# Building two adjacency matrices: 32 source blocks of 100 columns in place of 40 of 80, laps of 8 groups in place of 12

## The chip, the cores and the metric

The kernel runs on one core of one Trainium2 chip. The metric is device time in microseconds (us) of one execution. In this text PE is TensorE (PEld its weight loads), DVE is VectorE, ACT is ScalarE, POOL is GpSimd and SP is SyncE. A trailing q (DVEq, PEldq, SPq) means the instruction queue of the engine: register, branch, semaphore and DMA-issuing instructions, which are not counted as busy.

## The reference

A graph of 3125 nodes with 128 features and 103125 edges (sorted by destination) goes through four layers, each followed by an add and a layer norm: a weighted graph convolution, a graph attention layer with four heads, a dense attention over edges, and two mean aggregations with a hidden layer between. Cut to what matters here:

```
def _L0_gnn_ref(x, edge_row, edge_col, edge_val, weight, b):
    xw = x @ weight
    msgs = edge_val[:, None] * xw[edge_col]
    out = jax.ops.segment_sum(msgs, edge_row, num_segments=N_NODES)
    return jax.nn.relu(out + b)
...
x = _layernorm(x + _L0_gnn_ref(x, src, dst, edge_weight, ...))
x = _layernorm(x + _L1_gnn_ref(x, edge_index, ...))
x = _layernorm(x + _L2_gnn_ref(x, ..., edge_index))
x = _layernorm(x + _L3_gnn_ref(x, edge_index, ...))
```

All four layers sum over the edges of each destination. The kernel turns the edge list once into two dense matrices of 3200 x 3200 f32 in DRAM, row = destination and column = source: the number of edges, and the sum of their weights. Every layer then works from these.

## The kernel before, in words

`edge_tables` (L107) reads the edge list, and for every *group* of WD = 3 destination rows fetches 128 consecutive edges from the group's first edge on, one edge to a partition. Its loop over BATCHES (L331 to L338) unpacks them into the bf16 table `near`: for each group a field "key" (destination in the group times HI plus source block, 0 to KEYS-1), a field "low" (column in the block, 0 to SL-1), and the edge's weight split into PARTS = 3 bf16 numbers.

`build_matrices` (L420) makes the matrices. A row of 3200 columns is cut into HI = 40 source blocks of SL = 80, so a group of three rows has KEYS = 120 keys. The matrix product over the 128 edges of (one-hot of the key) and (one-hot of low, and the same times each part of the weight) gives a group's three rows as 120 partitions of 80 columns, for counts and weights at once. LW = 12 groups make a lap, and there are LAPS = 88 laps, run as a hardware loop of 44 with two laps in its body (`each_lap`, L445). Each lap goes through five engines:

- VectorE (`onehots`, L474): waits until the buffers of two laps ago are used, compares a grid with "low" for all 12 groups (L484, 960 elements), compares a grid with the key (L486, 1440 elements), waits for the first of the two, and multiplies by the three parts (L490, three times 960).
- TensorE (`products`, L517): per group three multiplications with the same stationary key one-hots of 128 columns (120 and 8 of zeros): moving 160 columns (low and first part), 80 and 80. The last of the lap's 36 is held back and issued after `beyond`.
- Between a lap's work and the next, VectorE's queue and TensorE's queue run `beyond` (L454): load two entries of the table `before_row` (L452), compare them and branch (L457). Only where a group has more than 128 edges is more work done; in this data the branch is never taken.
- ScalarE (`copy_out`, L556): copies the lap from PSUM into one of two staging buffers (L558), once the stores from that buffer have landed.
- SyncE (`store`, L565): two DMAs per lap (L568), counts and weights, each from 120 partitions with 12 runs of 80 f32 (320 bytes).

PSUM, the one-hot buffers and the staging buffers are all double. The order between the engines is set by the semaphores `used`, `lows`, `made`, `copied` and `stored`; nothing else runs in this stage. The 32 rows that the laps don't cover are zeroed by a separate DMA. The next stage (`aggregate`, L667) starts when the last store has landed.

Of the kernel before, what the change touches and what calls it, by code (L numbers as in the profile page):

```python
# [14 lines left out]
BF16 = mybir.dt.bfloat16  # L15
I32 = mybir.dt.int32
I16 = mybir.dt.int16
# [4 lines left out]
P = 128  # L22
# [23 lines left out]
WD = 3  # L46
HI = 40
SL = NP // HI
KEYS = WD * HI
LW = 12  # L50
LAPS = NP // (WD * LW)
ROWS = LAPS * LW * WD
# [54 lines left out]
def edge_tables(nc, k):  # L107

    with ExitStack() as ctx:
# [61 lines left out]
        N_PADS = 4  # L171
        N_CONSTS = 17
        BT = WT // BATCHES
# [35 lines left out]
        def _(pool):  # L209
# [10 lines left out]
            pool.memset(wrap[:, :], 0.0).then_inc(consts, 1)  # L220
            pool.memset(k.KEY[:, :, :, KEYS:P, :], 0.0).then_inc(consts, 1)
            pool.memset(k.zeros[:, :], 0.0).then_inc(consts, 1)
            pool.wait_ge(consts, 9)
            pool.affine_select(out=k.ident[:, :], in_=k.ident[:, :], compare_op=ALU.not_equal, fill=1.0,
# [8 lines left out]
            pool.iota(edge_i[:, :], pattern=[[P, ECOL]], base=0, channel_multiplier=1).then_inc(consts, 1)  # L233
            pool.iota(k.low_grid[:], pattern=[[1, SL], [0, 2]], base=0, channel_multiplier=0).then_inc(consts, 1)
            pool.iota(k.key_grid[:], pattern=[[1, KEYS], [0, 2]], base=0, channel_multiplier=0).then_inc(consts, 1)
            pool.wait_ge(rows_ready, 1)
# [11 lines left out]
            pool.iota(k.iota_low[:, :], pattern=[[1, SL]], base=0, channel_multiplier=0)  # L248
            pool.iota(k.iota_key[:, :], pattern=[[1, P]], base=0, channel_multiplier=0)
            pool.memset(nought[:, :], 0.0).then_inc(noughts, 1)  # L250

        @block.vector
        def _(dve):
# [166 lines left out]
def build_matrices(nc, k):  # L420


    with ExitStack() as ctx:
# [8 lines left out]
        more_key = sb("bm_more_key", [P, P], BF16)  # L432
# [3 lines left out]
        used, lows, made, copied, more_step, more_made, more_used = map(  # L436
            sem, ("bm_used", "bm_lows", "bm_made", "bm_copied", "bm_more_step", "bm_more_made", "bm_more_used"))
        stored = [sem(f"bm_stored{s}") for s in range(2)]
# [34 lines left out]
        def _(dve):  # L473
            dve.sem_inc(more_used, 1)  # L474

            def onehots(lap, u, two):
                wide_low, wide_key = [P, LW // 2, SL, 2], [P, LW // 2, KEYS, 2]

                def spread(f, wide):
                    return (k.near[:, f, bass.ds(lap * LW, LW)].rearrange("p (a b) -> p a b", b=2).unsqueeze(2)  # L480
                            .to_broadcast(wide))

                dve.wait_ge(used, lap + 1)
                dve.tensor_tensor(OH[:, u, :, 0], k.low_grid[:].unsqueeze(1).to_broadcast(wide_low),  # L484
                                  spread(1, wide_low), ALU.is_equal).then_inc(lows, 1)
                dve.tensor_tensor(k.KEY[:, u, :, 0:KEYS], k.key_grid[:].unsqueeze(1).to_broadcast(wide_key),  # L486
                                  spread(0, wide_key), ALU.is_equal)
                dve.wait_ge(lows, lap + 1)
                for v in range(PARTS):
                    last = dve.tensor_tensor(OH[:, u, :, 1 + v], OH[:, u, :, 0], spread(2 + v, wide_low), ALU.mult)  # L490
                last.then_inc(made, 1)

                def more(at, w, c, b, i):
# [3 lines left out]
                    dve.tensor_scalar(more_key[:], k.iota_key[:], k.key_base[:, bass.ds(w, 1)],  # L497
                                      k.col_key[:, bass.ds(c, 1)], ALU.add, ALU.is_equal).then_inc(more_step, 1)
# [13 lines left out]
        @block.tensor  # L512
        def _(pe):
            pe.sem_inc(used, RING)
            pe.sem_inc(copied, 2)

            def products(lap, u, two):  # L517
                def place(i, v):
                    b, c = divmod(i, PER_BANK)
                    return ps[:, 4 * u + b, c * WIDE + SL * (v > 0):(c + 1) * WIDE]  # L520

                def body(i, planes):
                    a, b = divmod(i, 2)
                    for v in planes:
                        moving = OH[:, u, a, 0:2, :, b] if v == 0 else OH[:, u, a, 1 + v, :, b]
                        last = pe.matmul(place(i, v), k.KEY[:, u, a, :, b], moving, start=i % PER_BANK == 0 and v == 0,  # L526
                                         stop=True, skip_group_check=True)
                    return last

                pe.wait_ge(copied, lap + 1)  # L530
                pe.wait_ge(made, lap + 1)
                for i in range(LW - 1):
                    body(i, range(PARTS))
                body(LW - 1, range(PARTS - 1))

                def more(at, w, c, b, i):
                    pe.wait_ge(more_made, at + 1)
                    for v in range(PARTS):
                        out = ps[:, bass.ds(b + 4 * u, 1), bass.ds(i * WIDE + SL * (v > 0), WIDE - SL * (v > 0))]
                        out = out.rearrange("p b c -> p (b c)")  # L540
                        last = pe.matmul(out, more_key[:], more_oh[:, 0:2] if v == 0 else more_oh[:, 1 + v],
                                         start=False, stop=True, skip_group_check=True)
# [1345 lines left out]
def program(nc, ins, out):  # L1888
# [15 lines left out]
    with ExitStack() as ctx:  # L1904
# [6 lines left out]
        with ExitStack() as edges:  # L1911
# [14 lines left out]
            k.iota_low = esb("iota_low", [P, SL], I16)  # L1926
            k.iota_key = esb("iota_key", [P, P], I16)
            k.low_grid = esb("low_grid", [P, SL, 2], I16)
            k.key_grid = esb("key_grid", [P, KEYS, 2], I16)
            k.KEY = esb("key_onehots", [P, RING, LW // 2, P, 2], BF16)  # L1930
            edge_tables(nc, k)
# [52 lines left out]
```

## Time and profile before

| | us |
|---|---|
| median of 3 runs (2443.68 to 2446.11) | 2445.59 |
| the profiled execution, its own time | 2446.72 |
| its span, first to last instruction | 2445.0 |
| TensorE busy | 1906.3 (78%) |
| VectorE busy | 1752.6 (72%) |
| ScalarE busy | 1135.5 (46%) |
| GpSimd busy | 137.2 (6%) |

The span is what the rows divide up; 1.7 us of the execution's own time lie outside it. The mean granted clock of TensorE is 0.894 of its full speed. The busy shares are averages over many stages; the build of the matrices is the stretch between about 80 and 478 us.

### The profile page before, as it was taken

What the parts mean: (1) busy time and instruction counts of PE and PEld (TensorE: products, weight loads), DVE (VectorE), ACT (ScalarE), POOL (GpSimd) and SP (SyncE); (2) the same over time, 40 slices, a digit from 0 to 9 for tenths busy, and PEclk for the clock granted to TensorE, in tenths of its full rate; (3) what the DMA queues carried; (4) which work ended last, traced back from release to release, by engine and by line L of the source; (5) the groups of instructions that cost most, each with busy time, mean ns of one, the idle gap of its engine ahead of it and who ended that gap; (6) DMA issues with size and microseconds to landing.
All of it is one profiled execution on the core that took longest, in us unless ns stands there. A gap on an engine that the chain in (4) does not pass through costs nothing. (4 is left out here: it accounts for less than half of the span.)

```text
span 2445.0 us, 44627 instructions
## 1 busy us (share of the span) xinstructions
PE 1906.3 (78%) x16121; PEld 1450.0 (59%) x16122; DVE 1752.6 (72%) x1874; ACT 1135.5 (46%) x1959; POOL 137.2 (6%) x225
## 2 busy tenths in 40 slices
PE   3456666499478888888888898873899999598794
PEld 2455555355357666666666776662688887354452
DVE  4777777400349999999999999846788876572374
ACT  1244444200156777667777776642666665101001
POOL 4000000000000000000000000000000000010120
PEclk7787777799789999999999999996899999699897
DMA  3599999997013333212333311220433330492492
GB/s 103 108 210 210 210 210 210 228 355 258 6 54 110 110 110 109 76 47 97 109 109 109 109 67 50 78 62 18 172 134 107 134 108 3 179 413 115 201 420 77
DMA packets 336138, 341.99 MB, mean 140 GB/s; under 512 B 267785, under 2 KB 318369, under 8 KB 319825
## 3 DMA queue, kind: packets, MB, share of 16 engines
q1 hardware_dynamic: 333712, 338.62, 43.0%
q0 software_dynamic: 720, 1.77, 0.3%
q10 hardware_dynamic: 1648, 0.83, 0.1%
q8 instruction: 37, 0.61, 0.1%
q14 instruction: 21, 0.16, 0.0%
HBM read 214.18 MB, written 127.01 MB: 140 GB/s over the span
## 5 line engine op out<-in xcount | busy, mean ns | idle before, releaser
L1201 ACT ACTIVATE exponentials<-gr_ps,att_cols 128x256 f32<-128x256 f32 (+1 forms) x1300 | 495.8, 490 | 203.0 <-PE gr_ps L1091 201.0
L1091 PE MATMUL gr_ps<-ident,gr_r 128*128 128x128 f32 x2500 | 381.4, 292 | 66.6 <-DVE gr_r L1309 64.4
L1122 PE MATMUL gr_ps<-exponentials,heads 128*33 128x128 f32 x5000 | 364.8, 277 | 15.3 <-DVE exponentials L1316 15.3
L1091 PEld LDWEIGHTS gr_ps<-ident,gr_r 128*128 128x128 f32 x2500 | 282.9, 146 | 150.7 <-issue 128.7
L1316 DVE SCALAR_TENSOR_TENSOR exponentials<-exponentials,gr_count_t 128x3072 f32<-128x3072 f32 (+1 forms) x104 | 349.6, 3361 | 22.4 <-ACT exponentials L1201 18.3
L526 PE MATMUL bm_ps<-bm_oh,key_onehots 128*128 128x80 bf16 (+1 forms) x3168 | 237.2, 243 | 163.9 <-issue 140.4
L1282 DVE CUSTOM_DVE_ANT_0 gr_unread<-gr_src_rows,gr_closed 128x3125 bf16<-128x3125 f32 (+1 forms) x100 | 344.6, 3446 | 15.1 <-ACT gr_closed L1194 14.5
L526 PEld LDWEIGHTS bm_ps<-bm_oh,key_onehots 128*128 128x128 bf16 x3168 | 210.6, 115 | 190.7 <-issue 178.9
L1122 PEld LDWEIGHTS gr_ps<-exponentials,heads 128*33 128x33 f32 x5000 | 255.0, 111 | 83.1 <-issue 56.8
L558 ACT ACTIVATE bm_stage<-bm_ps 120x1920 f32<-120x1920 f32 x88 | 155.8, 1771 | 249.4 <-DMA adjacency<-bm_stage 225.7
L790 PE MATMUL sage_ps<-sage_counts,sage_parts 128*128 128x400 bf16 x1200 | 207.7, 337 | 13.6 <-DVE sage_counts L824 13.6
L1309 DVE TENSOR_SCALAR gr_r<-gr_src_rows,gr_lift_u,gr_floor_u 128x3125 f32<-128x3125 f32 (+1 forms) x100 | 186.7, 1908 | 14.0 <-PE gr_ps L1091 8.4
L790 PEld LDWEIGHTS sage_ps<-sage_counts,sage_parts 128*128 128x128 bf16 x1200 | 118.7, 99 | 103.2 <-DVE sage_counts L824 15.1
L1542 PE MATMUL ar_ps<-KT,ar_left 128*128 128x400 f32 x400 | 147.1, 512 | 13.7 <-DVE ar_low_u L1633 12.1
L490 DVE TENSOR_TENSOR bm_oh<-bm_oh,near 128x960 bf16<-128x960 bf16 x264 | 157.5, 652 | 0.0
L1561 PEld LDWEIGHTS ar_ps<-ar_pt,X 128*128 128x128 f32 x1250 | 147.1, 194 | 11.5 <-ACT ar_pt L1605 4.5
L1561 PE MATMUL ar_ps<-ar_pt,X 128*128 128x128 f32 x1250 | 149.4, 277 | 0.0
L695 PE MATMUL agg_gcn_ps<-agg_gcn_ring,agg_gcn_left 128*128 128x400 f32 x400 | 136.0, 504 | 4.6 <-DMA agg_gcn_ring<-adjacency 4.6
L484 DVE TENSOR_TENSOR bm_oh<-low_grid,near 128x960 bf16<-128x960 int16 x88 | 58.0, 659 | 101.9 <-PE bm_ps L526 93.1
L824 DVE CAST sage_counts<-sage_ring 128x3200 bf16<-128x3200 f32 x50 | 93.7, 1874 | 46.4 <-POOL sage_ring L780 46.4
L1605 ACT ACTIVATE ar_pt<-ar_ps 128x512 f32<-128x512 f32 (+1 forms) x175 | 84.0, 547 | 79.1 <-PE ar_ps L1551 79.1
L1647 DVE CUSTOM_DVE_ANT_0 ar_p<-ar_p,ar_counts 128x1600 f32<-128x1600 f32 x50 | 89.3, 1823 | 42.5 <-ACT ar_p L1600 42.5
(319 smaller groups left out, 1908.0 us busy)
## 6 DMA issues: line engine op xcount, KB each, us to landing
sage_ring<-count_by_source SPq DMA_DIRECT2D x50, 1600.0 KB, 9.2
adjacency<-bm_stage SPq DMA_DIRECT2D x176, 450.0 KB, 5.6
agg_gcn_ring<-adjacency SPq DMA_DIRECT2D x25, 1600.0 KB, 8.5
gr_count<-adjacency SPq DMA_DIRECT2D x25, 1600.0 KB, 7.9
ar_counts<-adjacency SPq DMA_DIRECT2D x25, 1600.0 KB, 6.7
count_by_source<-gr_count_t SPq DMA_DIRECT2D x12, 3200.0 KB, 19.1
fg_node<-gat_node_sums SPq DMA_DIRECT2D x1, 1650.0 KB, 6.3
count_by_source<-gr_count_t SPq DMA_DIRECT2D x1, 1600.0 KB, 7.1
```

The lines of the kernel that those rows point to most:

```text
L490: last = dve.tensor_tensor(OH[:, u, :, 1 + v], OH[:, u, :, 0], spread(2 + v, wide_low), ALU.mult)
L526: last = pe.matmul(place(i, v), k.KEY[:, u, a, :, b], moving, start=i % PER_BANK == 0 and v == 0, stop=True, skip_group_check=True)
L558: act.activation(stage[:, u].rearrange("p (b w) v c -> p b (w v c)", b=BANKS), ps[0:KEYS, BANKS * u:BANKS * (u + 1), 0:PER_BANK * WIDE], A ...
L790: last = pe.matmul(ps[:, b, 0:CW], parts[:, u, i, :], counts[:, u, b * CW:(b + 1) * CW], start=False, stop=True, skip_group_check=True)
L1091: last = pe.transpose(ps[:, i % RINGS, c:c + P], r[:, j, s * P:(s + 1) * P], k.ident[:])
L1122: last = pe.matmul(ps[j * PAIR:j * PAIR + C + 1, 7, 0:P], heads[:, h, s, :], e[:, s, j * P:(j + 1) * P], start=s == 0, stop=s == NT - 1, s ...
L1201: last = act.activation(e[:, s, 0:w], ps[:, i % RINGS, c:c + w], ACT.Exp, bias=cols[:, h, s:s + 1])
L1282: dve.tensor_tensor_reduce(out=unread[:, 0:n], in0=src_rows[:, h, 0:n], in1=closed[:, j, 0:n], scale=1.0, scalar=FLOOR, op0=ALU.subtract, ...
L1309: last = dve.tensor_scalar(r[:, j, 0:n], src_rows[:, h, 0:n], lift_u[:, h, j:j + 1], floor_u[:, h, j:j + 1], ALU.add, ALU.max)
L1316: dve.scalar_tensor_tensor(part, part, 1.0, count_t[:, first:last, 0:w], ALU.min, ALU.mult).then_inc(weighed, 1)
L1542: last = pe.matmul(ps[:, b, 0:CW], left[:, u % RING, :], KT[:, cols], start=True, stop=True)
L1561: last = pe.matmul(ps[:, 7, 0:P], k.X[:, first + j, :], pt[:, i, j * P:(j + 1) * P], start=first + j == 0, stop=first + j == NT - 1, skip_ ...
```

## The change

The row is cut into 32 blocks of 100 columns: 96 keys, stores from 96 partitions with runs of 400 bytes. A lap has 8 groups, and there are 132 laps; the groups, their edges and the rows that the laps don't cover stay as they are. The key one-hots are made as wide as the low one-hots (100, of which 96 are copied out), in one buffer `hot` with the order plane, group, column. So one comparison makes the key plane and the low plane (1600 elements), and after a wait for it one multiplication makes the three weighted planes (2400 elements). `near` is laid out lap by lap, so that a lap's fields lie together. The stationary matrix of a multiplication has 100 columns in place of 128; the moving one has 200, 100 and 100 in place of 160, 80 and 80. GpSimd writes three constants fewer.

```
-HI = 40
+HI = 32
-LW = 12
-LAPS = NP // (WD * LW)
+LW = 8
+LAPS = 2 * (NP // (2 * WD * LW))
...
-                unpack(ids[:, cols], weight[:, cols], BW, k.near[:, 0, cols], k.near[:, 1, cols],
-                       [k.near[:, 2 + v, cols] for v in range(PARTS)], k.key_base[:, cols])
+                mine = [k.near[:, b * (BW // LW):(b + 1) * (BW // LW), f, :] for f in range(2 + PARTS)]
+                unpack(ids[:, cols], weight[:, cols], BW, mine[0], mine[1], mine[2:], k.key_base[:, cols])
...
-        OH = sb("bm_oh", [P, RING, LW // 2, 1 + PARTS, SL, 2], BF16)
+        hot = sb("bm_hot", [P, RING, 2 + PARTS, LW // 2, SL, 2], BF16)
...
-                dve.tensor_tensor(OH[:, u, :, 0], k.low_grid[:].unsqueeze(1).to_broadcast(wide_low),
-                                  spread(1, wide_low), ALU.is_equal).then_inc(lows, 1)
-                dve.tensor_tensor(k.KEY[:, u, :, 0:KEYS], k.key_grid[:].unsqueeze(1).to_broadcast(wide_key),
-                                  spread(0, wide_key), ALU.is_equal)
-                dve.wait_ge(lows, lap + 1)
-                for v in range(PARTS):
-                    last = dve.tensor_tensor(OH[:, u, :, 1 + v], OH[:, u, :, 0], spread(2 + v, wide_low), ALU.mult)
-                last.then_inc(made, 1)
+                dve.tensor_tensor(planes(both), k.grid[:].unsqueeze(1).to_broadcast(over(both)), spread(both), ALU.is_equal
+                                  ).then_inc(compared, 1)
+                dve.wait_ge(compared, lap + 1)
+                low = hot[:, u, 1].rearrange("p a c b -> p (a c b)").unsqueeze(1)
+                dve.tensor_tensor(planes(parts), low.to_broadcast([P, PARTS, LW * SL]), spread(parts), ALU.mult
+                                  ).then_inc(made, 1)
...
-                        moving = OH[:, u, a, 0:2, :, b] if v == 0 else OH[:, u, a, 1 + v, :, b]
-                        last = pe.matmul(place(i, v), k.KEY[:, u, a, :, b], moving, start=i % PER_BANK == 0 and v == 0,
-                                         stop=True, skip_group_check=True)
+                        moving = hot[:, u, 1:3, a, :, b] if v == 0 else hot[:, u, 2 + v, a, :, b]
+                        last = pe.matmul(ps[0:SL, BANKS * u + bank, c * WIDE + SL * (v > 0):(c + 1) * WIDE],
+                                         hot[:, u, 0, a, :, b], moving, start=c == 0 and v == 0, stop=True,
+                                         skip_group_check=True)
...
-            k.near = esb("near", [P, 2 + PARTS, NWP], BF16)
+            k.near = esb("near", [P, NWP // LW, 2 + PARTS, LW], BF16)
```

## Rows read from the trace of the kernel before

**Rows 1.** The page's busy slices, 40 of 61.1 us: the DMA row.
```profile
DMA  3599999997013333212333311220433330492492
```
**Rows 2.** ScalarE's copy out (L558): count, ns min/median/max, starts; what its idle time waited for.
```profile
L558 ACT ACTIVATE bm_stage<-bm_ps x88: 1770/1770/1774, 88.5 to 469.8; 120x1920 f32<-120x1920 f32 x88
...
  DMA adjacency<-bm_stage: 225.7, 86
```
**Rows 3.** The DMA view of the stretch 100 to 460 us.
```profile
DMA packets 238855, 75.65 MB, mean 210 GB/s; under 512 B 238855, under 2 KB 238855, under 8 KB 238855
```
**Rows 4.** Windows: us, then busy PE, PEld, DVE, ACT, POOL (count); PEclk, DMA share, GB/s.
```profile
300.00:400.00 100.00, 61.80 (x823) 55.02 (x824) 72.19 (x114) 39.78 (x24) 0.00 (x0) 0.77 0.93 210
92.20:94.00 1.80, 1.80 (x35) 1.65 (x35) 1.80 (x4) 1.35 (x1) 0.00 (x0) 1.00 0.85 186
301.50:304.70 3.20, 3.20 (x35) 3.02 (x35) 2.97 (x5) 1.58 (x1) 0.00 (x0) 0.52 1.00 212
```
**Rows 5.** VectorE's lines of a lap (L484, L486, L490), columns as in rows 2.
```profile
L484 DVE TENSOR_TENSOR bm_oh<-low_grid,near x88: 657/659/661, 81.3 to 459.2; 128x960 bf16<-128x960 int16 x88
L486 DVE TENSOR_TENSOR key_onehots<-key_grid,near x88: 900/901/905, 81.8 to 459.8; 128x1440 bf16<-128x1440 int16 x88
L490 DVE TENSOR_TENSOR bm_oh<-bm_oh,near x264: 649/652/656, 82.7 to 461.8; 128x960 bf16<-128x960 bf16 x132
```
**Rows 6.** TensorE's weight loads of the stage (L526), columns as in rows 2.
```profile
L526 PEld LDWEIGHTS bm_ps<-bm_oh,key_onehots x3168: 95/97/150, 84.6 to 466.7; 128*128 128x128 bf16 x198
```
**Rows 7.** VectorE's table loads (L452): 88 to 92 us, then 100 to 460 us.
```profile
L452 DVEq TENSOR_LOAD <-before_row x2: 304/306/307, 89.7 to 90.5; - x2
...
L452 DVEq TENSOR_LOAD <-before_row x164: 341/871/1390, 101.4 to 457.2; - x164
```
**Rows 8.** Queue instructions of one lap, 301.2 to 306 us (L531, L452, L490).
```profile
L531 PEldq EVENT_SEMAPHORE  x2: 51/51/51, 301.4 to 305.6; - x2
...
L452 PEldq FUSED_REGOPS  x4: 51/98/146, 303.0 to 304.9; - x4
L452 DVEq TENSOR_LOAD <-before_row x2: 894/912/930, 302.6 to 303.9; - x2
L452 PEldq TENSOR_LOAD <-before_row x2: 387/647/907, 303.1 to 303.9; - x2
...
L490 DVEq FUSED_REGOPS  x3: 57/57/57, 302.0 to 302.2; - x3
```
**Rows 9.** Timeline of the same lap: start us, us, engine, line, what [idle before].
```profile
301.29 0.66 DVE L484 TENSOR_TENSOR bm_oh<-low_grid,near 128x960 bf16<-128x960 int16 x1 [0.80 <-PE bm_ps L526]
...
301.48 3.26 PE L526 MATMUL bm_ps<-bm_oh,key_onehots 128*128 128x160 bf16 x35 [0.35 <-issue]
305.49 0.70 PE L526 MATMUL bm_ps<-bm_oh,key_onehots 128*128 128x80 bf16 x7 [0.75 <-issue]
...
305.95 0.66 DVE L484 TENSOR_TENSOR bm_oh<-low_grid,near 128x960 bf16<-128x960 int16 x1 [1.48 <-PE bm_ps L526]
```
**Rows 10.** The first laps: timeline, and VectorE's table loads of 81 to 84.5 us.
```profile
81.27 0.66 DVE L484 TENSOR_TENSOR bm_oh<-low_grid,near 128x960 bf16<-128x960 int16 x1 [0.96 <-PEq L514]
...
84.54 0.66 DVE L484 TENSOR_TENSOR bm_oh<-low_grid,near 128x960 bf16<-128x960 int16 x1
...
92.15 1.88 PE L526 MATMUL bm_ps<-bm_oh,key_onehots 128*128 128x160 bf16 x35 [0.41 <-DVE bm_oh L490]
...
L452 DVEq TENSOR_LOAD <-before_row x2: 316/434/553, 82.5 to 83.4; - x2
```
**Rows 11.** SyncE's stores (L568): issue ns min/median/max, and time to landing.
```profile
L568 SPq DMA_DIRECT2D adjacency<-bm_stage x176: 329/660/2111, 90.5 to 472.3; - x176
...
DMA to landing us min/median/max: 3.7/5.6/6.4
```
**Rows 12.** Timeline: VectorE's first large step.
```profile
11.55 0.63 DVE L289 CAST dst_f<-dst_i 128x903 f32<-128x903 int32 x1 [3.23 <-DMA dst_i<-in_dst_dram]
```
**Rows 13.** VectorE's conversions into `near` (L281, the same at L283).
```profile
L281 DVE CAST near<-weight x3: 359/359/360, 66.9 to 78.4; 128x384 bf16<-128x384 f32 x3
```

More of the change, by code:

```diff
@@ L171, in edge_tables @@
         N_PADS = 4
-        N_CONSTS = 17
+        N_CONSTS = 15
         BT = WT // BATCHES
@@ L220, in _ @@
             pool.memset(wrap[:, :], 0.0).then_inc(consts, 1)
-            pool.memset(k.KEY[:, :, :, KEYS:P, :], 0.0).then_inc(consts, 1)
             pool.memset(k.zeros[:, :], 0.0).then_inc(consts, 1)
-            pool.wait_ge(consts, 9)
+            pool.wait_ge(consts, 8)
             pool.affine_select(out=k.ident[:, :], in_=k.ident[:, :], compare_op=ALU.not_equal, fill=1.0,
@@ L233, in _ @@
             pool.iota(edge_i[:, :], pattern=[[P, ECOL]], base=0, channel_multiplier=1).then_inc(consts, 1)
-            pool.iota(k.low_grid[:], pattern=[[1, SL], [0, 2]], base=0, channel_multiplier=0).then_inc(consts, 1)
-            pool.iota(k.key_grid[:], pattern=[[1, KEYS], [0, 2]], base=0, channel_multiplier=0).then_inc(consts, 1)
+            pool.iota(k.grid[:], pattern=[[1, SL], [0, 2]], base=0, channel_multiplier=0).then_inc(consts, 1)
             pool.wait_ge(rows_ready, 1)
@@ L248, in _ @@
             pool.iota(k.iota_low[:, :], pattern=[[1, SL]], base=0, channel_multiplier=0)
-            pool.iota(k.iota_key[:, :], pattern=[[1, P]], base=0, channel_multiplier=0)
             pool.memset(nought[:, :], 0.0).then_inc(noughts, 1)
@@ L428, in sem @@
             return ctx.enter_context(nc.semaphore(name))
-        OH = sb("bm_oh", [P, RING, LW // 2, 1 + PARTS, SL, 2], BF16)
+        hot = sb("bm_hot", [P, RING, 2 + PARTS, LW // 2, SL, 2], BF16)
         gate = sb("bm_gate", [P, 1])
-        more_key = sb("bm_more_key", [P, P], BF16)
+        more_key = sb("bm_more_key", [P, SL], BF16)
         more_oh = sb("bm_more_oh", [P, 1 + PARTS, SL], BF16)
@@ L435, in build_matrices @@
         ps = ctx.enter_context(nc.psum_tensor("bm_ps", [P, 8, BANK], F32))
-        used, lows, made, copied, more_step, more_made, more_used = map(
-            sem, ("bm_used", "bm_lows", "bm_made", "bm_copied", "bm_more_step", "bm_more_made", "bm_more_used"))
+        used, compared, made, copied, more_step, more_made, more_used = map(
+            sem, ("bm_used", "bm_compared", "bm_made", "bm_copied", "bm_more_step", "bm_more_made", "bm_more_used"))
         stored = [sem(f"bm_stored{s}") for s in range(2)]
@@ L476, in onehots, with over, spread, planes @@
             def onehots(lap, u, two):
[L477 to L481, printed above, removed]
-                dve.wait_ge(used, lap + 1)
-                dve.tensor_tensor(OH[:, u, :, 0], k.low_grid[:].unsqueeze(1).to_broadcast(wide_low),
-                                  spread(1, wide_low), ALU.is_equal).then_inc(lows, 1)
-                dve.tensor_tensor(k.KEY[:, u, :, 0:KEYS], k.key_grid[:].unsqueeze(1).to_broadcast(wide_key),
-                                  spread(0, wide_key), ALU.is_equal)
-                dve.wait_ge(lows, lap + 1)
-                for v in range(PARTS):
-                    last = dve.tensor_tensor(OH[:, u, :, 1 + v], OH[:, u, :, 0], spread(2 + v, wide_low), ALU.mult)
-                last.then_inc(made, 1)
+                def over(fields):
+                    return [P, (fields.stop - fields.start) * (LW // 2), SL, 2]
+                def spread(fields):
+                    mine = k.near[:, bass.ds(lap, 1), fields].rearrange("p l f (a b) -> p (l f a) b", b=2)
+                    return mine.unsqueeze(2).to_broadcast(over(fields))
+                def planes(fields):
+                    return hot[:, u, fields].rearrange("p f a c b -> p (f a) c b")
+                both, parts = slice(0, 2), slice(2, 2 + PARTS)
+                dve.wait_ge(used, lap + 1)
+                dve.tensor_tensor(planes(both), k.grid[:].unsqueeze(1).to_broadcast(over(both)), spread(both), ALU.is_equal
[4 more added lines that the diff above has]
+                                  ).then_inc(made, 1)
                 def more(at, w, c, b, i):
@@ L496, in more @@
                                       ).then_inc(more_step, 1)
-                    dve.tensor_scalar(more_key[:], k.iota_key[:], k.key_base[:, bass.ds(w, 1)],
+                    dve.tensor_scalar(more_key[:], k.iota_low[:], k.key_base[:, bass.ds(w, 1)],
                                       k.col_key[:, bass.ds(c, 1)], ALU.add, ALU.is_equal).then_inc(more_step, 1)
@@ L517, in products @@
             def products(lap, u, two):
-                def place(i, v):
-                    b, c = divmod(i, PER_BANK)
-                    return ps[:, 4 * u + b, c * WIDE + SL * (v > 0):(c + 1) * WIDE]
                 def body(i, planes):
                     a, b = divmod(i, 2)
+                    bank, c = divmod(i, PER_BANK)
                     for v in planes:
-                        moving = OH[:, u, a, 0:2, :, b] if v == 0 else OH[:, u, a, 1 + v, :, b]
-                        last = pe.matmul(place(i, v), k.KEY[:, u, a, :, b], moving, start=i % PER_BANK == 0 and v == 0,
-                                         stop=True, skip_group_check=True)
+                        moving = hot[:, u, 1:3, a, :, b] if v == 0 else hot[:, u, 2 + v, a, :, b]
+                        last = pe.matmul(ps[0:SL, BANKS * u + bank, c * WIDE + SL * (v > 0):(c + 1) * WIDE],
+                                         hot[:, u, 0, a, :, b], moving, start=c == 0 and v == 0, stop=True,
+                                         skip_group_check=True)
                     return last
@@ L538, in more @@
                     for v in range(PARTS):
[L539 to L542, printed above, removed]
+                        out = ps[0:SL, bass.ds(b + BANKS * u, 1), bass.ds(i * WIDE + SL * (v > 0), WIDE - SL * (v > 0))]
+                        last = pe.matmul(out.rearrange("p b c -> p (b c)"), more_key[:],
+                                         more_oh[:, 0:2] if v == 0 else more_oh[:, 1 + v], start=False, stop=True,
+                                         skip_group_check=True)
                     last.then_inc(more_used, 1)
@@ L1926, in program @@
             k.iota_low = esb("iota_low", [P, SL], I16)
[L1927 to L1930, printed above, removed]
+            k.grid = esb("grid", [P, SL, 2], I16)
             edge_tables(nc, k)
```

## The prediction

> **What bounds the kernel now.** The change touches one stage, the build of the two adjacency matrices, so I first find it, then ask what sets its pace. Runs of this kernel that differ by less than 0.2% (4.9 us) cannot be told from no change.
>
> The busy slices [rows 1] show the stage as the flat stretch of 9s in the DMA row. ScalarE's copy of each lap starts between 88.5 and 469.8 us, 88 times [rows 2], so 87 lap periods take 381.3 us: 4.38 us a lap.
>
> The first reading is DMA. The stretch moves 210 GB/s, all of it in packets under 512 B [rows 3], at a share of 0.93 [rows 4], and ScalarE's idle time is put down to the stores, 225.7 us [rows 2]. 0.93 is 15/16 within rounding: fifteen engines that never rest and one that does nothing, as a store from 120 partitions would give if eight go to each engine. Per lap an engine then carries 2 x 1440 / 15 = 192 packets in 4.38 us, 22.8 ns for 320 B. The Trainium skill (DMA: Bandwidth & Descriptors, on why a DMA increments its semaphore by 16) says that a transfer uses the largest number up to 16 that divides its slowest dimension, 15 for 120 and 16 for 96; by that rule, the trace agrees.
>
> The second reading asks whether anything else leaves no room either. VectorE is busy 72.2 us of 100 and TensorE 61.8 [rows 4]. VectorE's waits are put down to TensorE, but TensorE's own to "issue" [rows 9], and that is the key: the gap is not a wait for data. Between its 35th and its 36th multiplication of a lap TensorE's queue runs the register program of `beyond`: two loads from a table, a comparison, a branch. VectorE's queue runs it too. These loads take 0.31 us before the first store moves and have a median of 0.87 us with the stores in flight [rows 7]; they are slowed by the DMA traffic. TensorE's semaphore wait starts at 301.4 and again at 305.6 [rows 8]: 4.2 us, of which 3.26 us of multiplications lie beside its two loads (0.387 and 0.907 us) and the rest of the program. The first register instruction starts at 303.0, before the 35 multiplications are over at 304.74. The last multiplication, which stands behind the branch, starts 0.75 us later at 305.49, for "issue" [rows 9].
>
> VectorE in the same place: comparison at 301.29, next one at 305.95 [rows 9], 4.66 us with loads of 0.894 and 0.930; without the loads 2.84. The first lap of all: 81.27 to 84.54 [rows 10], 3.27 us with loads of 0.553 and 0.316; without them 2.40. So a lap of VectorE's queue costs 2.62 us (the mean of a lap that ends in the loop's branch and one that does not) plus two loads: 4.36 us with loads of 0.87. That is the measured period again. Three things are full at once: fifteen DMA engines, TensorE's queue, VectorE's queue. The change enlarges the first and makes the other two run their fixed program 132 times in place of 88.
>
> **Part by part.**
> Laps: the groups stay 1056 (88 x 12, 132 x 8). All that is paid per lap is paid 1.5 times.
>
> VectorE's own work: 2.4 us busy per lap in place of 0.659 + 0.901 + 3 x 0.652 = 3.52 us [rows 5]. Between 960 and 1440 elements of a comparison lie 0.242 us, 0.504 ns an element; 1600 elements are 0.901 + 160 x 0.504 = 0.98 us, and the product of 2400 is 0.652 + 1440 x 0.504 = 1.38 us. Together 2.4 us; below the lap of its queue, so hidden by it. Should the longer patterns run at half the rate, 1600 x 0.504 = 0.8 us would come on top of the comparison, which the queue waits for.
>
> VectorE's queue: the wait for the comparison stands ahead of the product and of the register program. Today it lasts 0.66 us, since the key comparison and three products are queued around it; now 0.98 us (+0.33). Two product issues go, 0.13 us each (three starts from 302.0 to 302.2 [rows 8]), -0.26. Sum 2.62 + 0.07 = 2.69 us plus two loads. What is behind the waiting instruction is all of `beyond` and the next lap's comparison; TensorE waits for the product.
>
> TensorE: 24 multiplications a lap of 133 columns on average, in place of 36 of 107. Its queue began the register program 1.6 us into a lap [rows 8], when about 17 of the 35 were through at 3.26 / 35 = 0.093 us each; if 18 wait in front of the array again, it now begins after 5, at 0.7 us. So 4.2 - 1.3 (loads) - 0.9 = 2.0 us plus two loads: below VectorE's 2.69, and not the bound.
>
> DMA: 768 packets x 2 / 16 = 96 per engine and lap, of 400 B. Bounds: 22.8 ns if a packet costs the same whatever its size, 28.5 ns if it costs by the byte. That is 2.19 to 2.74 us a lap; I take the middle, 2.45. In 132 laps 323 us, against 386 us now: this is the gain that the change could have.
>
> ScalarE: 1600 elements, 1.50 us by 1771 x 1600/1920 rounded up; 198 us in all, no bound. SyncE's issues: 264 in place of 176, each with fewer packets; today's shortest is 0.329 us [rows 11], so 0.7 us of a lap, hidden by the DMA.
>
> The table loads: between 0.305 (DMA idle) and 0.87 us (DMA full) [rows 7]. In a lap of 4.0 us the DMA would be busy for 2.45, 61%, so I take 0.61 x 0.87 + 0.39 x 0.305 = 0.65 us. VectorE's queue then needs 2.69 + 1.30 = 3.99 us, which closes the circle: 4.0 us a lap.
>
> Outside the laps: three constants less on GpSimd; VectorE's first large step waits for the DMA of `dst` for 3.23 us after the last constant [rows 12], so that is worth 0. The batches write `near` in runs of 8 elements: six conversions of 0.36 us [rows 13] stay, or at worst double, 0 to +2.2 us; I take 0, since element count and types stay. VectorE's first lap of 3.27 us is 0.8 us shorter (3.52 busy less 2.4, with the wait between), the last copy 0.3 and the last stores 4.38 - 2.45 = 1.9: -3 us.
>
> Sum: 131 x 4.0 - 381.3 - 3 = +139.7 us. Against the profiled execution's own 2446.7 us that is 2586.4; that execution stands 1.1 us above the median of the runs, so the forecast is 2586 us. Ends: loads of 0.305 give 3.30 us a lap, +48 us, 2493; loads of 0.87 give 4.43 us, +196 us, 2642.
>
> **The rivals.**
> A, the stores pace the stage: the register programs run ahead of the engines and cost nothing. Then a lap is the longer of DMA (2.19 to 2.74) and VectorE (2.4): 131 x 2.4..2.74 - 381.3 - 3 = -70 to -25 us, 2376 to 2420, with the middle price (2.45) 2382. For it: share 0.93, and ScalarE that always waits for a store. Against it: the queue's lap without any DMA was 3.27 us [rows 10], and faster begins only below 2.91 us (381.3/131). Chance 0.04.
>
> B, the two staging buffers pace it. The first store landed 3.7 us after issue [rows 11]; less 2.19 us for 96 packets plus 2.45 us for a lap's two smaller stores 3.96, with the copy of 1.50 and 0.25 us of handing over 5.7 us for two laps, 2.86 each: -10 us, 2436 us. For it: with fewer bytes per buffer, the constant latency weighs more. Against it: the same 3.27 us. Chance 0.04; these constants are known to some 10 us in the sum, so half of it lies within 0.2% of before.
>
> C, TensorE's weight loads come into sight. 35 pairs take 1.88 us at 2.4 GHz (granted 1.00) and 3.26 at 1.2 GHz (0.52) [rows 4, 9, 10], 0.50 and 0.87 ns a column: a load of 0.097 us [rows 6] is hidden now. Were it exposed behind each of 23 multiplications of 0.067 (2.4 GHz) to 0.116 us, these would take 3.8 to 4.9 us, 4.3 at the mean clock of 0.77 [rows 4], and 0.4 to the next lap: 4.7 us, +231 us, 2677. Against it: 100 columns are fewer than 128. Chance 0.08. The Trainium skill (TensorE: Matmul & The Clock Gate, on fast weight load) says that the fast load needs exactly 128 columns, and that a load otherwise takes its columns over 1.2 GHz, here 83 ns; if those hide behind the multiplications, its sum is mine, if not, it is C.
>
> D, the comparison and the product run at half rate: 4.0 + 0.8 = 4.8 us, +245 us, 2690. Same types and same innermost pair as now speak against it. Chance 0.03.
>
> **The numbers.** My forecast has 0.81. The range takes its two ends, 2493 and 2642, raised to 2650 for what of C comes with smaller loads: outside are A, B, D and most of C, under 0.2. Faster: A and half of B, 0.06. Same: 0.02. Slower: 0.92.
>
> **What the profile after would show.** Right: a copy period near 4.0 us; DMA share near 0.6 with no flat 9s; ScalarE's idle time put down to TensorE, no longer to stores; table loads with a median between 0.5 and 0.8 us; VectorE busy under 65% of the stretch; a comparison of 0.98 and a product of 1.40 us. Wrong: a period under 3.2 us or a share above 0.9 (A); ScalarE still idle for stores at a period near 2.9 (B); 35 pairs' pace of over 0.1 us a pair at 2.4 GHz (C); a comparison over 1.5 us (D). Table loads that stay at 0.87 us with a share of 0.6 would put the period at 4.4.

## The result and the profile after

| | before | after |
|---|---|---|
| median of 4 runs each, us | 2445.85 | 2587.6 |
| lowest to highest, us | 2443.68 to 2446.43 | 2585.23 to 2588.6 |
| span of the profiled execution, us | 2445.0 | 2586.2 |

The ratio is 1.058 (95% interval 1.0562 to 1.0598): 142 us slower. The forecast was 2586 us.

The page's busy slices after (40 of 64.7 us); they answer to [rows 1]:
```profile
DVE  4666665552003899999999999985588887374275
DMA  3466666667841221122222222211233331194392
GB/s 97 95 153 154 153 155 153 154 153 253 318 150 54 103 97 64 67 86 103 103 103 103 103 103 103 76 31 32 106 125 127 124 107 49 56 418 197 143 422 94
```
The stretch of 9s in the DMA row has become one of 6s, at 154 GB/s in place of 210; everything to the right of it has kept its shape. The stage's own lines, answering to [rows 2, 5 to 7] (count, ns min/median/max, starts), each followed by what the engine's idle time before it waited for:
```profile
L556 ACT ACTIVATE bm_stage<-bm_ps x132: 1499/1499/1501, 87.2 to 611.9; 96x1600 f32<-96x1600 f32 x132
...
  PE bm_ps L523: 337.5, 128
  DMA adjacency<-bm_stage: 11.3, 4
...
L486 DVE TENSOR_TENSOR bm_hot<-grid,near x132: 991/992/994, 81.4 to 606.0; 128x1600 bf16<-128x1600 int16 x132
...
  issue: 191.6, 131
...
L490 DVE TENSOR_TENSOR bm_hot<-bm_hot,near x132: 1407/1407/1410, 82.5 to 607.2; 128x2400 bf16<-128x2400 bf16 x132
...
L523 PEld LDWEIGHTS bm_ps<-bm_hot x3168: 122/126/207, 84.1 to 611.5; 128*100 128x100 bf16 x198
...
L449 DVEq TENSOR_LOAD <-before_row x264: 301/642/1425, 82.7 to 608.4; - x132
...
L449 PEldq TENSOR_LOAD <-before_row x264: 298/307/1329, 84.8 to 610.2; - x132
```
131 periods in 611.9 - 87.2 = 524.7 us are 4.005 us each. ScalarE, which waited 225.7 us for stores before, now waits 337.5 us for TensorE and 11.3 for stores. VectorE's comparison waits for "issue", that is for its own queue, 131 times of 132. The trace's start times say the same: from the fifth lap on the comparison starts 47 or 48 ns after the last instruction of its queue, and never less than 1.17 us after TensorE was through with the buffer that it overwrites. The windows of before [rows 4] have this answer (us; busy PE, PEld, DVE, ACT, POOL; PEclk, DMA share, GB/s):
```profile
300.00:400.00 100.00, 59.10 (x600) 51.70 (x600) 59.99 (x50) 36.57 (x25) 0.00 (x0) 0.76 0.69 155
```
No engine is busy for more than 60% and the DMA for 69%: what paces the stage is none of them. The granted clock is 0.76 here and was 0.77 in the same window before, so the clock is not it either. The timeline of a lap, with VectorE's loads of the table in it:
```profile
301.28 0.99 DVE L486 TENSOR_TENSOR bm_hot<-grid,near 128x1600 bf16<-128x1600 int16 x1 [1.47 <-issue]
302.41 1.41 DVE L490 TENSOR_TENSOR bm_hot<-bm_hot,near 128x2400 bf16<-128x2400 bf16 x1
...
303.97 1.59 PE L523 MATMUL bm_ps<-bm_hot 128*100 128x200 bf16 x23 [1.07 <-DVE bm_hot L490]
305.11 0.99 DVE L486 TENSOR_TENSOR bm_hot<-grid,near 128x1600 bf16<-128x1600 int16 x1 [1.29 <-issue]
...
L449 DVEq TENSOR_LOAD <-before_row x2: 305/506/707, 302.5 to 303.6; - x2
```
Comparison (0.99), product (1.41) and then 1.29 us of nothing, in which the queue finishes its register program. 3.83 us less the two loads (0.305 and 0.707) leave 2.82 us; in the first lap the same sum is 2.45 us. Over all laps the trace has more: VectorE's 264 loads take 0.705 us in the mean, 1.41 us a lap, which leaves 2.59 us of the 4.005 for everything else in its queue.

### The profile page after: what moved, and what is told of

It is laid out like the page before. It is cut to its first block and busy times, and to the rows that moved or that the text cites. A ratio compares the mean times of both kernels' runs of the same rounds, so it can differ in the third digit from the quotient of the medians.

```text
span 2586.2 us, 45812 instructions
## 1 busy us (share of the span) xinstructions
PE 1983.4 (77%) x16121; PEld 1515.7 (59%) x16122; DVE 1789.0 (69%) x1698; ACT 1177.9 (46%) x2003; POOL 139.0 (5%) x222
## 3 DMA queue, kind: packets, MB, share of 16 engines
HBM read 214.18 MB, written 127.01 MB: 132 GB/s over the span
## 5 line engine op out<-in xcount | busy, mean ns | idle before, releaser
L523 PE MATMUL bm_ps<-bm_hot 128*100 128x100 bf16 (+1 forms) x3168 | 310.7, 262 | 235.1 <-DVE bm_hot L490 153.4
L523 PEld LDWEIGHTS bm_ps<-bm_hot 128*100 128x100 bf16 x3168 | 273.0, 156 | 273.1 <-issue 225.8
L556 ACT ACTIVATE bm_stage<-bm_ps 96x1600 f32<-96x1600 f32 x132 | 197.9, 1499 | 348.9 <-PE bm_ps L523 337.5
L486 DVE TENSOR_TENSOR bm_hot<-grid,near 128x1600 bf16<-128x1600 int16 x132 | 130.9, 992 | 192.6 <-issue 191.6
L490 DVE TENSOR_TENSOR bm_hot<-bm_hot,near 128x2400 bf16<-128x2400 bf16 x132 | 185.8, 1408 | 18.8
```

The lines of the kernel that those rows point to most:

```text
L490: dve.tensor_tensor(planes(parts), low.to_broadcast([P, PARTS, LW * SL]), spread(parts), ALU.mult).then_inc(made, 1)
L523: last = pe.matmul(ps[0:SL, BANKS * u + bank, c * WIDE + SL * (v > 0):(c + 1) * WIDE], hot[:, u, 0, a, :, b], moving, start=c == 0 and v = ...
L556: act.activation(stage[:, u].rearrange("p (b w) v c -> p b (w v c)", b=BANKS), ps[0:KEYS, BANKS * u:BANKS * (u + 1), 0:PER_BANK * WIDE], A ...
```

## The experiments

All times stand beside runs of the kernel before on the same chip, whose medians were 2444.67, 2445.28 and 2444.38 us in the three groups. Where no interval is given there was one timed run. A period is the time from the first copy's start to the last one's, divided by the laps between. What follows the last copy's start took 1969 to 1985 us in these traces, so single runs are best compared by their periods.

**Without the register program, on both engines.**
```
-                beyond(dve, lap, more)
...
-                beyond(pe, lap, more)
```


> The changed kernel without beyond on VectorE and TensorE (the look whether a group of the lap has more than 128 edges; in this data the branch is never taken, so the result stays). My theory: the register program with its two table loads paces the lap of 4.0 us through VectorE's queue. Without it a lap is set by what comes next: the stores (share 0.69 of 4.0 us = 2.76 us), VectorE's 0.99 + 0.15 + 1.41 = 2.6 us, or the two staging buffers (2.9 to 3.0): a period of 2.8 to 3.0 us, -130 to -160 us against the changed kernel, 2430 to 2460 us, with the DMA share above 0.9. Rival, the multiplications with 100 stationary columns or the longer steps of VectorE pace it: the period stays above 3.6 us, 2535 us or more.

2503.8 us, 84 us less than with it. The copies start every (532.9 - 86.2) / 131 = 3.41 us. That the register program was on the path is confirmed; the slow end of my sum (2460 us) was still 44 us faster than the chip. The windows from 100 to 400 us, and then the waits (us in total, times, longest):
```profile
100.00:400.00 300.00, 181.50 (x2106) 170.13 (x2107) 209.41 (x176) 132.02 (x88) 0.00 (x0) 0.84 0.80 180
...
ACT bm_stage L554 <- DMA adjacency<-bm_stage: 235.1, 123, 3.2
PEld bm_ps L522 <- ACT bm_stage L554: 189.6, 123, 2.6
```
The share is 0.80, not above 0.9, yet ScalarE waits for a landing 123 times: a wait for latency in the ring of two staging buffers, with engines to spare.

**The same on the kernel before.** The same two lines are taken out of the kernel before.

> The kernel before without beyond on both engines. My theory, three things full at once: fifteen DMA engines hold the period at 4.38 us, so the time stays within 0 to -8 us of before (2438 to 2446 us), TensorE and VectorE begin to wait in their queues, and the table loads' slowness is gone with them. Rival, the share of 0.93 is chance and the queues alone paced the kernel before: VectorE's work of 3.5 us and TensorE's of 2.9 on average would set a period of 3.5 us, -75 us, 2370 us.

2441.3 us, ratio 0.9986 (0.9976 to 0.9996). The period went from 4.38 to 4.34 us. DMA is the firm bound of the kernel before; the register program took 0.04 us a lap there, though both queues ran nearly without a pause. My reading, which no run tests, is that the longer table loads only filled time that was there.

**Laps of 8 alone.**
```
-LW = 12
-LAPS = NP // (WD * LW)
+LW = 8
+LAPS = 2 * (NP // (2 * WD * LW))
```


> The kernel before with laps of 8 groups (132 laps) alone: 40 blocks of 80, stores from 120 partitions, three products and two comparisons as before. My theory, the number of laps is what costs: VectorE's queue has a fixed 2.62 us less 0.16 for the shorter comparison, plus two loads of 0.6 to 0.75, so a period of 3.7 to 4.0 us, +100 to +143 us, 2546 to 2589 us; stores 128 packets x 22.8 ns = 2.9 us, a share of 0.7 to 0.75. Rival, the geometry (96 partitions, 400-byte runs, 100 columns) or the joined comparison is what made the change slower: then laps of 8 alone cost under 30 us.

2549.9 us, +105 us against before, period 3.74 us. Three quarters of the loss needs no new geometry. VectorE's loads take 1.34 us of the period and the rest of its queue 2.40 us, where the changed kernel has 1.41 and 2.59: that is the 0.27 us between the two periods. The profile has the signs of the changed kernel:
```profile
100.00:400.00 300.00, 197.86 (x1924) 168.45 (x1921) 181.95 (x402) 98.99 (x80) 0.00 (x0) 0.50 0.74 164
...
ACT bm_stage L558 <- PE bm_ps L526: 344.1, 131, 20.1
DVE bm_oh L484 <- issue: 191.2, 130, 2.4
```
TensorE was granted 0.50 of its clock here and 0.77 in the changed kernel, but its pace isn't the lap's: the first comparison of a lap starts 46 or 47 ns after its own queue's last instruction, at least 0.95 us after TensorE was through with the buffer.

**Without it on VectorE only.** The first of the two lines of the first experiment.

> The changed kernel without beyond on VectorE only; TensorE keeps it. My theory: VectorE's queue falls out of the path and TensorE's takes over, 2.0 to 2.2 us fixed plus two loads of 0.45 to 0.8: a period of 3.0 to 3.6 us, 2455 to 2535 us. Rival, the two queues wait for each other in series (the pair paces, not VectorE's alone): removing one would then save at most its own loads' half, a period above 3.6 us.

2511.4 us, period 3.43 us: 76 of the 84 us come from VectorE's queue alone, and of the other 8 the periods (3.426 and 3.409 us) account for only 2. TensorE, with its register program in place, holds next to nothing up: ScalarE again waits for stores (232.3 us, 119 times), as in the first experiment.

**Two comparisons in the changed kernel**, low first, and the wait for that one.
```
+                dve.tensor_tensor(planes(lows), ..., spread(lows), ALU.is_equal).then_inc(compared, 1)
+                dve.tensor_tensor(planes(key), ..., spread(key), ALU.is_equal)
-                dve.tensor_tensor(planes(both), ..., spread(both), ALU.is_equal).then_inc(compared, 1)
```


> The changed kernel with the comparison taken apart again: low (800 elements) first, then the key (800), and the wait before the product is for the first. My theory: the queue waits for 0.58 us in place of 0.99 and issues one instruction more (0.13), so the fixed part falls by 0.28 us a lap, with somewhat slower loads up to a third of it given back: -25 to -37 us against the changed kernel, 2550 to 2563 us. Rival, the wait lies beside something else (TensorE's part of the lap): no change, 2583 us or more.

2513.8 us, 74 us less: one instruction more per lap makes the kernel faster, and by twice what I forecast. The key's comparison is issued while the first one runs and so costs the queue nothing; the comparison that the queue waits for takes 0.576 us in place of 0.992, and the queue's part without the loads falls by 0.38 us, to 2.21. The other third of the gain is shorter loads, 0.61 us in the mean in place of 0.705, where I had expected longer ones:
```profile
L557 ACT ACTIVATE bm_stage<-bm_ps x132: 1499/1500/1503, 87.9 to 537.4; 96x1600 f32<-96x1600 f32 x132
...
L449 DVEq TENSOR_LOAD <-before_row x264: 300/498/1371, 83.1 to 532.7; - x132
...
ACT bm_stage L557 <- DMA adjacency<-bm_stage: 245.4, 126, 4.4
```
ScalarE waits for stores here too, so 3.43 us is at the same time where the staging ring stands; the queue alone might have gone lower. TensorE's granted clock was 0.99 in this run, 0.77 in the changed kernel and 0.86 in the run before this one, which has the same period; so I don't put the gain down to the clock.

**Loads first, four staging buffers.**
```
+                at_ends = ends(dve, lap)       # VectorE: after the comparison is issued
                 dve.wait_ge(compared, lap + 1)
...
+                at_ends = ends(pe, lap)        # TensorE: ahead of its waits
                 pe.wait_ge(copied, lap + 1)
```


> The changed kernel with four staging buffers and a loop body of four laps, and with the two table loads of a lap issued earlier: on VectorE between the comparison and the wait for it, on TensorE ahead of its waits; the comparison of the two values and the branch stay where they were. My theory: VectorE's queue no longer pays the wait for the comparison (0.99 us) and the loads (1.41 us on average) one after the other but beside each other, and the staging ring (3.4 us a lap in the run without the register program) is gone: a period of 2.9 to 3.1 us, 2440 to 2465 us. Rival, the loads' own slowness grows with a fuller DMA (0.87 us each): a period of 3.2 us or more, 2475 us.

2529.7 us, period 3.55 us: far from my theory. The rival's number holds (3.2 us or more), its reason doesn't: the loads take 0.67 us (VectorE) and 0.76 us (TensorE) in the mean, not 0.87. The waits are on both sides:
```profile
ACT bm_stage L567 <- PE bm_ps L533: 290.0, 132, 21.6
...
DVE bm_hot L498 <- issue: 87.1, 67, 2.5
```
On TensorE my edit was wrong. Where its loads stood before, they ran beside the multiplications that were already waiting in front of the array; now they stand behind the whole lap's and ahead of the next one's waits. In the lap at 302.25 us the multiplications run until 303.89, the first load (0.70 us) lies beside them, the second (1.12 us) lies at 304.2 to 305.3 beside nothing, and the next multiplications start at 305.82. In 98 of the last 128 laps TensorE starts more than 0.2 us after VectorE's product is ready. VectorE's product is late for "issue" 67 times too, as two slow loads outlast the comparison. ScalarE waits 290.0 us for TensorE, all 132 times, and for no store. How much is due to each of the two queues is not separated, as loads first on VectorE alone was not tried.

**Four staging buffers, no register program.**
```
+STAGES = 4
...
-            with eng.Fori(0, LAPS // 2) as two:
-                for u in range(2):
+            with eng.Fori(0, LAPS // STAGES) as two:
+                for u in range(STAGES):
```


> The changed kernel without beyond and with four staging buffers (loop body of four laps). My theory: after the register program the ring of two staging buffers was the next wait, 3.41 us a lap at a share of 0.80. With four the sixteen engines fill up: 96 packets at 28.4 ns, a period of 2.75 to 2.9 us at a share above 0.93, 2425 to 2440 us. Rival, the ring was not the wait but the DMA's rate with 400-byte packets from two stores at a time: the period stays above 3.2 us, 2475 us or more.

2490.3 us, 50 us above my theory, period (503.8 - 86.1) / 131 = 3.19 us. The ring was the wait, since 0.22 us a lap went with it. But here the sixteen engines are full, and they move less than fifteen did:
```profile
100.00:400.00 300.00, 178.84 (x2258) 167.50 (x2256) 223.50 (x188) 139.44 (x93) 0.00 (x0) 0.90 0.97 192
```
192 GB/s at a share of 0.97 (0.93 to 1.04 over the stretches of 100 us), against 210 at 0.93. A packet of 400 bytes costs 16 x 0.97 x 3.19 / 1536 = 32.2 ns in the mean, more than the 28.5 ns of my upper bound. It is a mean with a tail: in the trace's packet records from 100 to 400 us the median is 24 ns in this run and in the changed kernel alike, but here 2% of the packets take over 100 ns and hold 12% of the time, where the changed kernel has next to none. So even with nothing but the stores in the way, this geometry gives 132 x 3.19 = 421 us where the old one gives 386. The gain that the change was to bring is not hidden by something else; it is not there.

**One look for the whole table**, with four staging buffers. Nothing is left out; the choice is made once, on VectorE as shown and on TensorE in the same way.
```
+            with dve.If(any_beyond(dve)):
+                each_lap(dve, lambda *at: onehots(*at, True))
+            with dve.Else():
+                each_lap(dve, lambda *at: onehots(*at, False))
```


> As the run before, but with nothing left out: VectorE and TensorE each compare the first and the last entry of the table once ahead of their loops, and take a loop with beyond in it where any group of all has more than 128 edges, else a loop without. My theory: the same time as without beyond within 3 us, 2425 to 2443 us, so at last a little faster than before (0.2 to 0.8%). Rival: the 16 engines' gain is eaten by something that the larger program adds (instruction fetch of two loops): above 2446 us.

2489.1 us, ratio 1.0179 (1.0162 to 1.0196), equal to the run before it, and again some 46 us above what I had expected. The look ahead of the loop shows only in the first copy, which starts at 90.8 us in place of 86.1. The version gives back 98 of the 142 us; of the 44 that are left, 39 are the period of 3.21 us, which the stores set.

**Matrices 16 bytes further on.**
```
-    adj = dram("adjacency", (2, NP * NP))
+    adj = dram("adjacency", (2, NP * NP + 64))[:, 4:4 + NP * NP]
```


> The kernel before with both matrices, writers and readers alike, placed 16 bytes further on in DRAM, so that every 320-byte run of the stores starts and ends inside a 64-byte piece and touches six pieces in place of five. A theory formed on the runs so far: with its DMA full the changed kernel paid 32.2 ns for a 400-byte packet, which always touches seven such pieces (4.6 ns each), and the kernel before 22.8 ns for five (4.56 ns each), so the price goes by the 64-byte pieces touched. Then a packet costs 27.4 ns here, a lap 192 x 27.4 = 5.26 us, +77 us, 2522 us, plus a little for the readers. Rival one, the price goes by the number of engines (16 full ones get less each than 15): no change, 2446 us. Rival two, pieces that are only partly written cost a read and a write more: above 2560 us.

2900.9 us: 456 us slower, with the same packets of the same size. **The control**, 16 in place of 4 elements:

> The control: the same matrices 64 bytes further on, so that every run still covers five whole pieces. All theories that go by 64-byte pieces: no change, 2441 to 2450 us. Were the price set by larger pieces (256 or 512 bytes) or by the odd place of the readers' rows, it would be slower, above 2455 us.

2445.4 us, no change. The windows of the two from 100 to 400 us, the one with 16 bytes first, and its copies:
```profile
100.00:400.00 300.00, 107.53 (x1107) 96.43 (x1108) 96.64 (x153) 54.91 (x31) 0.00 (x0) 0.57 0.96 95
```
```profile
100.00:400.00 300.00, 186.35 (x2477) 165.57 (x2475) 218.35 (x344) 120.69 (x69) 0.00 (x0) 0.76 0.93 210
```
```profile
L558 ACT ACTIVATE bm_stage<-bm_ps x88: 1771/1771/1777, 87.3 to 920.8; 120x1920 f32<-120x1920 f32 x88
...
L452 DVEq TENSOR_LOAD <-before_row x176: 302/308/1418, 81.3 to 890.5; - x176
```
The DMA is as busy as ever (0.96) and moves 95 GB/s in place of 210; the period is 9.58 us. A 320-byte packet that starts and ends inside a 64-byte piece costs 16 x 0.96 x 9.58 / 2880 = 51 ns in the mean, not 22.8. So where a run begins does count. The control says less than it seems to: 320-byte runs begin at 0, 64, 128 and 192 bytes past a multiple of 256 in turn, and moving them by 64 only exchanges these places. It shows that the move itself costs nothing as long as each boundary stays on a multiple of 64; whether 64 or a size below it (32) is the one that counts, and whether 256 would be better, it doesn't tell. But my rule (4.6 ns for each piece touched) gave 27.4 ns and fell; the second rival, a price for pieces that are only partly written, is the one whose number holds. Its mechanism is not shown, and a fixed price on each such packet doesn't fit: every packet of this stage now has partly written ends, yet the median packet still takes 20 ns, as in the kernel before. The whole difference is a tail. A tenth of the packets take over 100 ns and hold 47% of the time, while before none took more than 76. So some packets are held up for long, and by what is open. The page's total of bytes read from HBM is the same 214.18 MB in all of these profiles, so whatever is done more is not counted there.

**Laps of 8 without the register program, old geometry.**

> The kernel before with laps of 8 groups and without beyond: 120 partitions, 320-byte runs, two staging buffers. It tells whether the 3.41 us a lap of the changed kernel without beyond came from the smaller lap (constant latencies in the ring of two staging buffers) or from the 400-byte runs. Theory, the ring's constants: 3.2 to 3.5 us a lap, 2470 to 2510 us, at a DMA share of 0.8 to 0.87. Rival, the runs' size: the stores' own 128 x 22.8 ns = 2.92 us set the period, 2435 to 2445 us, share 0.93.

2458.2 us, period 3.05 us, share 0.91: between the two theories. The small lap itself costs 14 us against before (18 by the periods). The changed kernel's 3.41 us, also without the register program, is 0.36 us a lap more, 46 us in all. ScalarE waits for stores in both, so this belongs to what passes through the staging ring: the 400-byte runs from 96 partitions, whose landing has a median of 4.2 us in place of 4.0, and the longer copy (1.50 us in place of 1.24). The two were not separated; the joined comparison has no part in it.

**One look, kernel before.** The same edit as above, on the kernel before.

> The kernel before with laps of 12 and the look for groups of more than 128 edges taken once ahead of the loops (two loops in the program, one with beyond and one without; nothing left out). Theory: as without beyond, the fifteen DMA engines hold the period at 4.34 us: 2438 to 2444 us, 0.1 to 0.2% faster than before. Rival: the second loop's code costs what that gains: no change.

2443.4 us, ratio 0.9991 (0.9982 to 1.0): no difference that counts, 0.2% being the bound. The period is 4.34 us as without the register program, and the first copy starts 2.1 us later. It is the best that I have with nothing left out; no version found clearly beats the kernel before.

## Why the prediction was right, and where its steps were not

**The step that carried it holds.** "A lap of VectorE's queue costs 2.69 us plus two loads": it is 2.59 plus 2 x 0.705 us. Taking the register program off that one queue gives back 76 us, taking it off both 84. VectorE's queue paused nowhere; its comparison was late for "issue". TensorE's queue was not the bound, as said.

**The lap count as the cost.** Laps of 8 alone: +105 us with the register program, +14 without. So about 91 us of the old geometry's loss are the program run 132 times. The remaining 37 of the 142 us lie in VectorE's queue as well, with a period of 4.005 in place of 3.74: the wait for the joined comparison, and somewhat longer loads. The stores have no part in them, since ScalarE waited for stores only 4 times. These costs don't simply add: each run shows what is left when the one ahead of it is gone (4.00, then 3.41 for the ring, then 3.19 for the stores).

**Terms that were off.** A load was put at 0.65 us and took 0.705 in the mean; the rest of the queue was put at 2.69 and took 2.59. The two errors cancel (+0.11 and -0.10 us a lap), and the hit within 2 us is luck beyond what the working can claim. The working itself gives 2585.3 us from the median of the runs; 2586 is its sum from the profiled execution, which is 1.1 us longer. The way to the 0.65, a mix of 0.305 and 0.87 by the DMA share, is not how loads behave here. They fall into two groups. In the changed kernel, 145 of TensorE's 264 loads begin while the DMA engines are less than 10% busy (in the first 0.3 us of the load) and take 0.305 us in the mean, and 66 begin while these are over 80% busy and take 0.87; of VectorE's, 144 fall in such busy stretches, at 1.02 us, and the rest take 0.33. That is why TensorE's median is 0.307 (mean 0.47) beside VectorE's 0.642. And with the matrices 16 bytes further on, the share is 0.96 but the median load of VectorE 0.308 us, so a busy DMA alone doesn't make a load slow.

**Terms that were right, and the weight loads.** The comparison (0.992 for 0.98) and the product (1.407 for 1.38) were right to 2%. The first multiplications of a lap come at 1.59 / 23 = 0.069 us each, as computed (0.067); the weight loads take 0.126 in place of 0.097 us and stay hidden, so rival C is out. The Trainium skill (TensorE: Matmul & The Clock Gate, on fast weight load) has the condition of 128 columns, by which the load of 100 loses the fast mode. The trace agrees in the direction, but not with the 83 ns that the prediction worked out from the Trainium skill, and no run here tests the condition by itself.

**The DMA term failed.** I took 2.45 us a lap (25.5 ns a packet) between 22.8 and 28.5. In the changed kernel it was 16 x 0.69 x 4.005 / 1536 = 28.8 ns, at the top, where the price by the byte is, and with full engines 32.2. Both ends came from counts of bytes and packets; that a 400-byte run starts off a 64-byte boundary three times in four did not enter. Whether that, the sixteenth engine or the fuller queue makes the 32.2 is not shown; that the 320-byte runs of before, at a share of 0.93, have no packet over 76 ns speaks for the place of the runs. It did no harm to the forecast, since the stores were hidden, but it made the gain that I thought was masked (63 us) out of a loss. The Trainium skill (DMA: Bandwidth & Descriptors, on the number of engines) is borne out by the share of 0.97: sixteen engines do work for 96 partitions. On the price of a run, the Trainium skill (DMA: Bandwidth & Descriptors, How a descriptor splits into AXI transactions) has a rule that I had passed over: a transfer that doesn't begin on a multiple of 256 bytes is fetched from the one below, in beats of 32. The Trainium skill says this of what is read; taken over to the places that these stores write, it gives an estimate. A 320-byte run of before has 13 beats in the mean over its places and a 400-byte run 16.5, which makes 22.8 x 16.5 / 13 = 28.9 ns: the 28.8 of the changed kernel, but so does the plain price by the byte (28.5), and the 32.2 beside full engines is neither. For the runs moved by 16 bytes the estimate is 14 beats or 24.6 ns, and the run showed 51, so it isn't what made those dear.

**The rivals.** A asked for a period under 3.2 us and a share above 0.9: neither. B had the right mechanism and the wrong size: the ring gives 3.41 us, not 2.86, once the queue is out of the way; a first store lands after 3.3 us at the least, where I had worked out 2.7. D fell with the comparison's 0.99 us.

**Signs named in advance**: period near 4.0 (4.005), ScalarE waiting for TensorE, VectorE under 65% (60), loads between 0.5 and 0.8 (0.64). The share was to be near 0.6 and was 0.69, for the reason above.

## What to carry to other kernels

An instruction queue is a resource like an engine: where the idle time is put down to "issue", add up the queue's own instructions and waits over a lap before changing how many laps there are, and keep waits and table loads out of its path. Joining two instructions can lengthen a lap if a wait behind them now covers both. Before trading partitions against bytes per run in a store, look at where each run starts: 320-byte runs moved off multiples of 64 bytes brought the store rate from 210 to 95 GB/s here, a larger step than any that run length or the number of engines made. And look at the spread of the packets' times beside their mean: an unchanged median with a long tail says that some packets are held up, not that all cost more.

## What I had not expected of the hardware

- Moving 320-byte runs by 16 bytes raises their mean cost from 22.8 to 51 ns and the kernel's time by 456 us, while the median packet stays at 20 ns; moving them by 64 bytes changes nothing (2445.4 us).
- Sixteen engines with 400-byte runs move 192 GB/s, fifteen with aligned 320-byte runs 210. Why a 400-byte run (32.2 ns, three boundaries in four inside a piece) suffers so much less than a shifted 320-byte run (51 ns, every boundary inside one) stays open: it was not tried which packets meet in a piece, nor at what time.
- A queue's table load has a minimum of 0.30 us and a median of 0.87 us in the kernel before, at 210 GB/s; in the changed kernel it depends on when in the lap it falls (TensorE's median 0.307 beside VectorE's 0.642 in the same laps). At a share of 0.96 but 95 GB/s VectorE's median is 0.308. One load of the first lap took 0.553 us before the first store was issued, so the stores are not all that can slow it.
